# A wait ahead of GpSimd's first gather of selected rows, in a one-core audio tower with eight experts

## What is computed

```python
h = dct(frames(x))                                   # (32, 938, 128)
h = h + recurrence(layernorm(h), nu, theta, gamma)   # long convolution along the frames
h = h + ffn(layernorm(h))

def ffn(x):                                          # E = 8, F = 512, C = 1024
    x_flat = x.reshape(N, 128)                       # N = 30016
    probs = softmax(x_flat @ Wr, axis=0)             # over the frames, for each expert
    vals, idx = top_k(probs.T, C)                    # (8, 1024)
    selected = x_flat[idx]
    h = gelu(einsum('ecd,edf->ecf', selected, W1) + b1[:, None, :])
    out_e = einsum('ecf,efd->ecd', h, W2) + b2[:, None, :]
    weighted = vals[..., None] * out_e
    return zeros_like(x_flat).at[idx.reshape(-1)].add(weighted.reshape(-1, 128))
```

## Time and profile before

| | |
|---|---|
| median of 3 runs | 606.38 us |
| lowest and highest run | 602.31, 607.04 us |
| span of the profiled execution | 605.3 us |
| VectorE busy | 425.8 us (70%) |
| TensorE busy | 397.3 us (66%) |
| GpSimd busy | 298.7 us (49%) |
| ScalarE busy | 292.2 us (48%) |

### The profile page before, as it was taken

The page is one execution under the profiler, slowest core; times in us unless marked ns, Lnnn a source line. Parts: engine busy times, 40 slices in busy tenths (PEclk is TensorE's granted clock), DMA queues, the critical chain, the costliest instruction groups (busy, mean ns, idle before and its releaser), DMA issues.

```text
span 605.3 us, 11347 instructions
## 1 busy us (share of the span) xinstructions
PE 397.3 (66%) x3577; PEld 320.0 (53%) x3577; DVE 425.8 (70%) x1653; ACT 292.2 (48%) x560; POOL 298.7 (49%) x213
## 2 busy tenths in 40 slices
PE   5798898999888889997000033210199989997900
PEld 5786788865877788764000022110057667775700
DVE  3877878898488887898888878911787658866100
ACT  2787840076699740177545500120258667686400
POOL 0467830058478730076000007776235687888774
PEclk9999999999899999999555555555579989999965
DMA  8679606699888227699999501121011344443332
GB/s 162 132 183 272 150 15 162 142 253 241 194 148 148 58 48 157 201 275 254 323 318 318 190 0 44 49 52 48 17 28 61 67 74 67 65 75 44 31 30 22
DMA packets 86116, 77.44 MB, mean 128 GB/s; under 512 B 15022, under 2 KB 82930, under 8 KB 85810
## 3 DMA queue, kind: packets, MB, share of 16 engines
q1 hardware_dynamic: 68674, 64.52, 41.6%
q0 software_dynamic: 10368, 8.40, 9.8%
q10 hardware_dynamic: 7024, 3.89, 2.7%
HBM read 52.27 MB, written 39.39 MB: 151 GB/s over the span
## 4 chain that ended last, share of the span: by engine, by line
PE 32%; DVE 21%; issue 14%; DMA 10%; POOL 10%; ACT 6%; another core or an unknown queue 5%; SPq 1%; ACTq 1%; DVEq 0%; POOLq 0%
PE banks L1003 7%; POOL out L1843 7%; PE banks L1030 5%; PE banks L929 5%; PE banks L1133 4%; PE banks L1146 4%; PE banks L1040 3%; DMA xin<-in_x 3%; ACT xn L680 2%; PE banks L915 2%; DMA ring<-toeplitz 2%; DVE xn L1512 2%; DMA const<-constants 1%; DVE xn L1576 1%
## 5 line engine op out<-in xcount | busy, mean ns | idle before, releaser
L1829 POOL DMA_INDIRECT hid<-kept,index x64 | 65.0, 1015 | 115.6 <-DVE index L1624 97.0
L1214 DVE BATCH_NORM_STATS2 stats<-hid 120x6 f32<-120x128 f32 (+1 forms) x512 | 104.9, 278 | 19.8 <-ACT hid L671 19.4
L1843 POOL DMA_INDIRECT out<-hid,index x56 | 88.6, 1582 | 25.9 <-issue 16.3
L929 PE MATMUL banks<-const,xt 128*120 128x128 f32 x512 | 74.0, 290 | 12.0 <-ACT xt L666 11.5
L775 ACT ACTIVATE xt<-banks 128x480 f32<-128x480 f32 x64 | 36.3, 570 | 84.9 <-PE banks L1030 83.7
L929 PEld LDWEIGHTS banks<-const,xt 128*120 128x120 f32 x512 | 63.9, 192 | 20.7 <-ACT xt L666 14.4
L1751 POOL TENSOR_TENSOR small<-small,powers 120x16 f32<-120x16 f32 (+2 forms) x18 | 47.9, 2662 | 47.1 <-DVE small L1232 47.1
L1819 POOL TENSOR_TENSOR small<-small,powers 120x16 f32<-120x16 f32 x15 | 43.2, 2901 | 41.7 <-DVE small L1232 36.3
L1003 PE MATMUL banks<-xn,ring 122*120 122x128 f32 x512 | 58.9, 276 | 6.3 <-DMA xn<-s 3.1
L1146 PEld LDWEIGHTS banks<-w_ring,xn 128*128 128x128 f32 x512 | 60.5, 196 | 3.9 <-issue 3.9
L1003 PEld LDWEIGHTS banks<-xn,ring 122*120 122x120 f32 x512 | 57.6, 189 | 7.4 <-issue 6.9
(11 more groups left out here) (222 smaller groups left out, 705.1 us busy)
## 6 DMA issues: line engine op xcount, KB each, us to landing
kept<-out SPq DMA_DIRECT2D x1, 15008.0 KB, 50.5
xin<-in_x SPq DMA_DIRECT2D x28, 480.0 KB, 6.9
out<-hid SPq DMA_DIRECT2D x14, 960.0 KB, 11.1
w_ring<-in_L_ffn_W SPq DMA_DIRECT2D x16, 256.0 KB
ring<-toeplitz SPq DMA_DIRECT2D x32, 112.5 KB
toeplitz<-ring SPq DMA_DIRECT2D x6, 545.0 KB, 11.3
out<-hid SPq DMA_DIRECT2D x2, 784.0 KB
xin<-in_x SPq DMA_DIRECT2D x4, 384.0 KB
```

The lines of the kernel that those rows point to most:

```text
L929: mm = pe.matmul(banks[0:L, 2 + n % 4, i * D:(i + 1) * D], xt[:, n % 2, i, :], cut["basis_t"], start=True, stop=True)
L1214: ins = dve.bn_stats(stats[:, slot, b, :], hid[:, bass.ds(c * HB + b, 1), :].rearrange("p a k -> p (a k)"))
L1829: pool.indirect_dma_start(found[:, n, :], None, kept, bass.IndirectOffsetOnAxis(ap=index[:, n:n + 1], axis=0)).then_inc(found_in[e], 16)
L1843: pool.indirect_dma_start(rows, at_rows, adds[:, n, :], None, compute_op=ALU.add, oob_is_err=True, bounds_check=ROWS * FRAMES - 1).then_in ...
```

## The change

A second wait is put ahead of GpSimd's first gather: for the row numbers of experts 0 to 5, which is twelve halves. The order of all instructions on all engines stays the same.

```diff
@@ -59,6 +59,7 @@
 FOUND_FIRST = 54
 WEIGHED_AFTER = {3: (3, 5), 5: (5, 7), 6: (7, 8)}
 FOUND_BETWEEN = 2
+ROWS_KNOWN = 12
 COPIED_ROWS = 512
 RING, SLOTS = 8, 4
 TURN = RING * SLOTS
@@ -1848,6 +1849,7 @@
 
 
             pool.wait_ge(kept_in, 16)
+            pool.wait_ge(index_ready, ROWS_KNOWN)
             for n in range(FOUND_FIRST):
                 find(n)
             n = FOUND_FIRST
```

## The result

The kernel after takes 630.9 us, the median of 3 runs (630.12 to 634.71), against 606.38 before: ratio 1.043, 95% interval 1.038 to 1.048. It is slower by about 24.5 us, four times what the forecast said (612.2), inside the range, and close to rival B (627). The profiled execution is one of 630.12 us with a span of 628.3. That is 23.0 more than the span before, and 1.8 us of the time lie outside the span. All lines stand one further down in the file than before (the gathers are line 1830, the choice 1615 to 1625).

What follows compares the result with a forecast made beforehand. GpSimd's own queue was taken to set the end from 476.17 to the last addition. +6.68 - 0.84 = +5.84 us on the 605.3 us span gave 611.1, with 1.1 around it 612.2 us; range 606 to 633.

Steps and rivals of the forecast that it cites:

- rival B: Lateness moves along into the new gather run, holding up expert 0's arithmetic: 15.2 us over forecast, 627 us; chance 0.15.
- Step 1: Wait before the first gather: experts 4 and 5 chosen punctually by 399.28, first gather at 400.19.
- Step 2: GpSimd's 54 gathers: 67.39 us plus 1.96 for slow ones, through at 469.54.
- Step 3: Expert 0's additions and two gathers: data ready at 442.8, so expert 1's additions start at 482.85, 6.68 us later.
- Step 4: GpSimd's tail: the wait for expert 3's data before its additions goes, 0.84 us back; two landing waits stay.
- Step 5: TensorE idles longer before expert 7, its clock may drop: taken as 0, at worst 6.4 us to the end.
- the expert 7 slack: Expert 7's first four tiles are ready at 573.16, GpSimd reaches them at 582.91: 9.75 us of slack.
- Rivals C: Lateness in choosing experts 4 and 5 is unrelated to gathers: first gather 428.61, all 28.4 us later, 641 us; chance 0.12.
- the partial case: One or two of the choice's three late increments stay; with one 11.6 us wait left, 624 us; chance 0.07.
- D: Arithmetic from expert 7's last gather, not GpSimd's queue, sets the end: its 16.6 us gain comes out, 590 us; chance 0.06.
- the sign that the arithmetic is the bound: A pause of over 1 us in GpSimd's tail where data comes late; it would show the forecast wrong.

Runs made afterwards that it cites:

- known8: Kernel after with the wait ahead of the first gather shortened from twelve halves to eight (experts 0 to 3): 618.8 us, ratio 1.021 to the kernel before.
- plain_no_wait: Kernel before with each gather replaced by a plain copy of 128 fixed rows on the same queue: 575.24 us, ratio 0.954 to the kernel before.
- first40: Kernel before with 40 gathers, not 54, ahead of the additions, four, not two, between experts, paired landing waits after 24 gathers: 612.77 us, ratio 1.018.
- plain: Kernel after with each gather replaced by a plain copy of 128 fixed rows on the same queue: 581.52 us, ratio 0.959 to the kernel before.
- rows64: Kernel after with each gather fetching only rows 0 to 63, the other half set to zero beforehand: 644.81 us, ratio 1.064 to the kernel before.
- drain: Kernel after with a wait for the newest gather's landing behind the 16th, 32nd and 48th gather: 628.24 us, ratio 1.036 to the kernel before.
- paced: Kernel before with GpSimd waiting at every second of the first 54 gathers until both have landed: 622.15 us, ratio 1.028 to the kernel before.
- first24: Kernel after with 24 gathers, not 54, ahead of the first addition and eight, not two, between experts' additions: 633.78 us, no ratio given.
- spaced: Kernel before with a small memset on GpSimd and a wait for it behind each of the first 54 gathers: 591.59 us, ratio 0.981.

## Why the prediction was wrong where it was

Step 1, the end of the wait: right. The choice of experts 4 and 5 was over at 399.91 (forecast 399.28), the first gather at 400.82 (400.19). The reason that I gave for it, that no gathers run beside the choice any more, is more than it takes: in known8 gathers do run beside it, at full beat but begun only 10 us before, and the choice is punctual; with copies in place of gathers it is, too (397.95 + 0.16 in plain_no_wait).

Step 2, the gathers: right in kind, small in size. They are through at 470.10 + 1.25 = 471.35 instead of 469.54. 0.63 us of the 1.81 is the later start. The rest is the slow gathers: the one at 418.60 took 2.86 us beside pair 3's scan and alone costs 1.9, what I had put down for all; two more beside the marks on VectorE took 1.13 and 1.19. The rule of the Trainium skill that I had weighed there (SBUF — State Buffer, "SBUF: two separate sides") says that VectorE in a 2-port mode locks GpSimd out. My "agrees" said too much. The gathers at 367.84 and 418.60 both stand beside a scan of 2.16 us that began within 0.1 us of them, and both are 1.9 us longer than usual, which fits a lock. But that the scan runs in a 2-port mode no row shows: it takes 2.16 us for 960 elements, where a TENSOR_SCALAR on 1024 of the same type takes 0.42 (1.67 for four).

Step 3, expert 0's additions: this is the step that failed, in its sentence "Their data is ready". The moments came at 412.39, close to the 411.5 that I had worked out, but the data came only just ahead of the first addition at 479.81, not at 442.8. I had carried the 31.3 us from the moments to the first addition (428.09 to 459.38) over from a stretch in which nine gathers started, in two groups, into one with 44 in a row; it took 67.4 (412.39 to 479.81). In the prediction's terms the overlap was wrong: I put the price of gathers beside expert 0's arithmetic at nothing, and it was 36.1 us. By the terms of the sum: 1.8 from step 2, 8.77 - 0.30 = 8.5 idle before the first addition, 3.87 - 0.30 = 3.6 before expert 1's, together 13.9 more than the 482.85 forecast for these (496.79).

Step 4, the tail: the sign was wrong. The 1.14 us idle before expert 3's additions became 3.00 instead of going, 2.7 more than forecast, and 0.57 before expert 4's (at 553.23) adds 0.3. With 5.84 forecast that makes 5.84 + 13.9 + 2.7 + 0.3 = 22.7 of the 23.1 us by which the last addition is later.

Step 5, the clock: no part of it. The granted clock is at the lower level of 1.2 GHz (0.50) in 450:460, when TensorE does four matmuls, but the expert 7 slack that I feared for was not touched: the two waits before the last experts are for landings (2.58 us at 588.33 and at 606.01).

Rival B is what happened: late from 433 (forecast 432.2), released at 475.4 (474.1), first addition at 479.8 (484.7), 630.9 us (627). Part of the closeness is luck. B let nothing be done during the hold-up and left 10.6 us of arithmetic for after it, where it was 4.4; and it had none of the 3.6 and 2.7 us by which the later additions waited longer, which made up for that. That the lateness began 32 us after the first gather, as in the kernel before, is no rule either: it was 21 in known8. I gave B 0.15. Its evidence was in the trace: the first 32 us of the old run were clean, and a wait of 4.22 us had come back behind two gathers. What I held against it, six gathers from 443.55 on without any such wait, was no evidence, since those six lasted 7.5 us and followed a pause of 10.89. And I took "nothing but gathers ran when the increments were late" as a reason to expect punctual increments after the wait, when it was the reason to expect late ones wherever the gathers went.

Rivals C and the partial case are out: the choice has no late increment left. D's 590 us is out. Its mechanism is not wholly: the queue does wait for expert 0's, 1's and 3's answers, which the prediction had named as the sign that the arithmetic is the bound, only that the answers came later and not earlier. first40 shows the point at expert 7 from which the arithmetic decides, too. That the queue was the bound is true only while nothing is held up. The rule "Issue the DMA early, do compute, wait on its semaphore late" (the Trainium skill, DMA: Bandwidth & Descriptors, "Rules for kernel authors"), which I had weighed against the change, has its own price in plain beside plain_no_wait, where the first addition comes 7.35 us later; in the times it is 3 to 6 us and not clear of the noise. That fits the rule, and it is the small part of the 24.5.

What stays open is the mechanism. Shown is that it takes gathers in place of copies (plain has none of it; whether for GpSimd's work or for the scattered rows isn't told apart), that spreading them makes it later and less (1.25 us from one to the next; 1.39: less; pairs with landings at some 2.2: none in the run), that fewer rows and bytes don't lessen it (rows64), and that three pauses for landings don't end it (drain). Whether the additions, which are indirect DMAs too, take part isn't shown: they stand beside the late waits in paced and first24, but plain has them at the same places without any. Why it begins only after some time, 21 to 63 us in these runs and not the same in two executions of the same instructions, isn't shown. Every run here has a recorded span, so no run tells either whether the writing of the records is part of it.

## What to carry to other kernels

When increments are late beside one engine's long uninterrupted series, ask first where that series will stand after the change, and lay the lateness on whatever stands there; moving the series moves the cost, and here onto expert 0's arithmetic, which the first additions, and so the whole queue behind them, wait for. A slower beat can be faster: one small memset and its wait behind each of 54 gathers gave 1.9%. And when work is moved behind the first of a queue's outputs, count it against what that output gains (first24, first40).

## What the runs showed of the hardware

A gather of 128 rows on GpSimd takes 1.248 us from one to the next, one of 64 rows 1.208, and a plain copy of 128 rows 0.55 (29.47 / 54).

When a series of gathers has run at 1.25 us for some 21 to 37 us, TensorE, VectorE and ScalarE are held up together, also in instructions that wait for nothing that the profile shows. Not all are: eight normalisations in a row on ScalarE kept their 0.40 us each (452.88). Their records then fall on a common raster of 0.70 us: VectorE at 440.37, 441.06 and 442.47, TensorE at 457.18, 459.98 and 462.79, whose distances are 1, 2, 4 and 4 times 0.70 (and 21 times between the two engines). Two engines often go on at the same moment: ScalarE at 440.39 beside the 440.37, both of them at 469.49 and at 475.09 in rows64. It looks like one thing that the engines wait for, but no run isolates it. Increments seem to wait as well: expert 0's came 22.9 us after the last record of its matmuls. GpSimd itself isn't held up (eight gathers in each 10 us), and the traffic goes on (52 GB/s). The hold-up ends 5.3 us after the last gather's start in the kernel after (475.38) and 0.9 us after it in spaced (439.81 behind 438.88).
